# Two-layer attention kernel: two sets of accumulated sums, three buffers of low parts, and another place for the join and the first seed

## What is computed

```python
# layer 0, per image b: xf = x as [128 channels, 4096 positions]
g_x, theta_x, phi_x = g_w @ xf + g_b, theta_w @ xf + theta_b, phi_w @ xf + phi_b   # 64 channels each
y = softmax(theta_x.T @ phi_x, axis=-1) @ g_x.T
x = W_w @ y.T + W_b + xf
# layer 1, on the result
q, k, v = Wq @ xf + bq, Wk @ xf + bk, Wv @ xf + bv                                 # 128 channels
x = x + (softmax(q.T @ k / sqrt(128), axis=-1) @ v.T).T
```

## Time and profile before

| | us |
|---|---|
| median of 3 runs | 3351.05 |
| lowest and highest | 3350.34, 3352.49 |
| the profiled execution | 3353.0 |
| its span, first to last instruction | 3351.2 |
| PE busy / POOL busy in it | 3245.4 / 2854.9 |

### The profile page before, as it was taken

One profiled execution on the slowest core, in us unless ns is written; L12 is line 12 of the kernel. 1 busy time (PEld: TensorE's weight loads), 2 busy tenths in 40 slices (PEclk: granted clock), 3 DMA queues, 4 the chain that ended last, 5 costly groups with the idle time before them and its releaser, 6 DMA issues. The chain is left out here.

```text
span 3351.2 us, 38415 instructions
## 1 busy us (share of the span) xinstructions
PE 3245.4 (97%) x13636; PEld 2198.1 (66%) x13636; DVE 2094.0 (62%) x3036; ACT 1902.4 (57%) x2473; POOL 2854.9 (85%) x1419
## 2 busy tenths in 40 slices
PE   8999999999999999999999999999999999999997
PEld 5555555557777765555777776555677777677775
DVE  5555555557767665555767675555677767677773
ACT  4455455556666655555666665545565666656564
POOL 6888888888888889898888888888888888888886
PEclk9999999999999999999999999999999999999998
DMA  1000000004656640000665653000165656556565
GB/s 52 24 20 26 23 26 26 26 26 101 136 116 136 128 97 19 24 26 26 133 131 113 138 113 88 26 23 26 37 135 110 140 123 132 120 109 137 107 132 110
DMA packets 64271, 271.41 MB, mean 81 GB/s; under 512 B 7120, under 2 KB 7120, under 8 KB 39504
## 3 DMA queue, kind: packets, MB, share of 16 engines
q0 software_dynamic: 27648, 201.34, 29.7%
q1 hardware_dynamic: 36432, 67.62, 6.7%
HBM read 50.83 MB, written 16.78 MB: 20 GB/s over the span
## 5 line engine op out<-in xcount | busy, mean ns | idle before, releaser
L921 DVE TENSOR_REDUCE piece_max<-rough 128x1 f32<-128x512 f32 x2032 | 1315.7, 684 | 654.3 <-PE rough L509 648.1
L384 POOL TENSOR_TENSOR sums<-sums,probs 128x1024 f32<-128x1024 f32 x448 | 1066.3, 2380 | 139.3 <-ACT probs L838 100.9
L1040 POOL TENSOR_TENSOR p_lo<-probs,p_hi 128x1024 fp32r<-128x1024 f32 x448 | 1135.9, 2668 | 11.2 <-ACT probs L832 11.1
L938 DVE TENSOR_TENSOR probs<-scores,shift_rows 128x1024 f32<-128x1024 f32 x512 | 626.4, 1223 | 541.9 <-PE scores L542 539.6
L838 ACT ACTIVATE probs<-scores 128x1024 f32<-128x1024 f32 x512 | 520.6, 1024 | 684.2 <-PE scores L536 683.7
L831 ACT ACTIVATE p_hi<-probs 128x1024 fp32r<-128x1024 f32 x448 | 474.4, 1059 | 586.9 <-DVE probs L938 586.8
L509 PE MATMUL rough<-keys_a,qry_a 128*128 128x512 f32 x2032 | 706.6, 416 | 35.5 <-DVE piece_max L921 20.0
L509 PEld LDWEIGHTS rough<-keys_a,qry_a 128*128 128x128 f32 x2032 | 368.1, 188 | 349.8 <-DVE piece_max L921 219.3
L832 ACT ACTIVATE probs<-probs 128x1024 f32<-128x1024 f32 x512 | 535.9, 1047 | 99.1 <-DVE probs L938 99.1
L538 PE MATMUL scores<-qry_a,keys_a 128*128 128x512 f32 x1024 | 448.8, 438 | 0.0
L533 PE MATMUL scores<-qry_a,keys_a 128*128 128x512 f32 x1024 | 432.5, 422 | 0.0
(11 more groups left out here) (94 smaller groups left out, 3183.7 us busy)
## 6 DMA issues: line engine op xcount, KB each, us to landing
sent_sums<-probs POOLq DMA_DIRECT2D x192, 1024.0 KB, 6.9
x_q<-x SPq DMA_DIRECT2D x32, 256.0 KB, 2.7
x_res<-x SPq DMA_DIRECT2D x32, 256.0 KB, 3.0
mid<-mid_new SPq DMA_DIRECT2D x32, 256.0 KB, 2.3
x_kv<-mid SPq DMA_DIRECT2D x32, 256.0 KB, 2.7
x_q<-mid SPq DMA_DIRECT2D x32, 256.0 KB, 2.7
x_res<-mid SPq DMA_DIRECT2D x32, 256.0 KB, 5.4
out<-result SPq DMA_DIRECT2D x32, 256.0 KB, 5.2
```

The lines of the kernel that those rows point to most:

```text
L384: eng.tensor_tensor(sums[:], sums[:], probs[:, slot(st, s)], ALU.add).then_inc(s_plus, 1)
L921: nc.vector.reduce_max(piece_max[:, t, c:c + 1], src, AX.X).then_inc(s_reduced, 1)
L938: nc.vector.tensor_tensor(probs[:, slot(st, s)].rearrange("p (h c) -> p h c", c=QB), scores[:, s % 2].rearrange("p (h c) -> p h c", c=QB), ...
L1040: nc.gpsimd.tensor_tensor(dst, w, rd(hi), ALU.subtract).then_inc(done, 1)
```

## The change

It does four things.

- `sent_sums` exists twice, for even and for odd blocks (`st.parity`). Seeds, sends and the fold take the block's own pair. A seed waits for the fold of two blocks before in place of the one before. Layer 0's `sums` is now the first half of the even pair, and its first add waits for a fold where the block before is of layer 1.
- `p_lo` has three buffers (`LO_BUFS`), taken in the order of the split groups, and each split waits for `s_used`: PE must have used the group three splits back.
- The fold between two layer-1 blocks stands at step 3, not 2.
- The first seed stands at step 1, not 2.

```diff
@@ -22,6 +22,7 @@
 SHARED_BUFS = 2
+LO_BUFS = 3
 HI_SLOTS = (2, 3, 0, 1)
...
-FOLD_AT = {None: (None, None), 0: (1, 1), 1: (3, 2)}
+FOLD_AT = {None: (None, None), 0: (1, 1), 1: (3, 3)}
...
-SEED_AT = {2: 0, 3: 2}
+SEED_AT = {1: 0, 3: 2}
...
-        p_lo = sb("p_lo", [P, len(HI_SLOTS), GC], F32R)
+        p_lo = sb("p_lo", [P, LO_BUFS, GC], F32R)
...
-        sums = sb("sums", [P, GC])
-        sent_sums = sb("sent_sums", [P, TPG, GC])
+        sent_sums = sb("sent_sums", [P, 2, TPG, GC])
+        sums = sent_sums[:, 0, 0]
...
+        def lo_part_of(nth, s):
+
+            return p_lo[:, (halved(nth, s) - 1) % LO_BUFS]
...
-        def fold(eng, layer, g, nth):
+        def fold(eng, layer, g, nth, parity):
...
-                eng.tensor_tensor(sent_sums[:, 0], sent_sums[:, 0], sent_sums[:, 1], ALU.add).then_inc(s_join, 1)
+                both = sent_sums[:, parity]
+                eng.tensor_tensor(both[:, 0], both[:, 0], both[:, 1], ALU.add).then_inc(s_join, 1)
...
             if s == 1:
-                if st.prev == 0:
-                    eng.wait_ge(s_fold, st.g)
+                if st.prev is not None:
+                    eng.wait_ge(s_fold, st.g - (st.prev == 1))
...
-                    mm(acc_out[:, parity], hi, p_lo[:, s % len(HI_SLOTS), at], start=False, stop=False)
+                    mm(acc_out[:, parity], hi, lo_part_of(nth, s)[:, at], start=False, stop=False)
...
             def split_probs(st, s):
                 pool.wait_ge(s_whole, whole_of(st.g, s))
-                lo_part(p_lo[:, s % len(HI_SLOTS)], probs[:, slot(st, s)], hi_part(s), s_p_lo)
+                n = HALVED.index(s) - LO_BUFS
+                if n >= 0:
+                    pool.wait_ge(s_used, used(st.g, HALVED[n]))
+                elif st.prev == 1:
+                    pool.wait_ge(s_used, used(st.g - 1, HALVED[n]))
+                lo_part(lo_part_of(st.nth, s), probs[:, slot(st, s)], hi_part(s), s_p_lo)
 
             def seed(st, s):
 
                 pool.wait_ge(s_whole, whole_of(st.g, s + 1))
-                if st.prev == 1:
+                if st.prev == 0:
                     pool.wait_ge(s_fold, st.g)
-                nc.gpsimd.tensor_tensor(sent_sums[:, s // 2], probs[:, slot(st, s)], probs[:, slot(st, s + 1)],
+                else:
+                    pool.wait_ge(s_fold, st.g - 1)
+                nc.gpsimd.tensor_tensor(sent_sums[:, st.parity, s // 2], probs[:, slot(st, s)], probs[:, slot(st, s + 1)],
                                         ALU.add).then_inc(s_seed, 1)
...
-                nc.gpsimd.dma_start(sent_sums[:], probs[:, first:first + TPG], accum_op=ALU.add).then_inc(s_sent, 16)
+                nc.gpsimd.dma_start(sent_sums[:, st.parity], probs[:, first:first + TPG], accum_op=ALU.add).then_inc(s_sent, 16)
```

More of the change, by code:

```diff
@@ L365, in fold @@
                 eng.wait_ge(s_sent, sent(nth, GROUPS - 1))
-                eng.tensor_tensor(sent_sums[:, 0], sent_sums[:, 0], sent_sums[:, 1], ALU.add).then_inc(s_join, 1)
+                both = sent_sums[:, parity]
+                eng.tensor_tensor(both[:, 0], both[:, 0], both[:, 1], ALU.add).then_inc(s_join, 1)
                 eng.wait_ge(s_join, nth + 1)
-                halves = sent_sums[:, 0, 0:QB], sent_sums[:, 0, QB:GC]
+                halves = both[:, 0, 0:QB], both[:, 0, QB:GC]
             eng.wait_ge(s_den, g + 1)
@@ L378, in add @@
             if s == 1:
-                if st.prev == 0:
-                    eng.wait_ge(s_fold, st.g)
-                eng.tensor_tensor(sums[:], probs[:, slot(st, 0)], probs[:, slot(st, 1)], ALU.add).then_inc(s_plus, 1)
+                if st.prev is not None:
+                    eng.wait_ge(s_fold, st.g - (st.prev == 1))
+                eng.tensor_tensor(sums, probs[:, slot(st, 0)], probs[:, slot(st, 1)], ALU.add).then_inc(s_plus, 1)
                 return
             eng.wait_ge(s_plus, added(st.nth, s - 1))
-            eng.tensor_tensor(sums[:], sums[:], probs[:, slot(st, s)], ALU.add).then_inc(s_plus, 1)
+            eng.tensor_tensor(sums, sums, probs[:, slot(st, s)], ALU.add).then_inc(s_plus, 1)
         def halved(nth, s):
@@ L1028, in block_program @@
                 if st.ends:
-                    fold(dve, st.layer, st.g, st.nth)
+                    fold(dve, st.layer, st.g, st.nth, st.parity)
                     reciprocals(st.g, st.parity)
@@ L1098, in block_program @@
                     if s == FOLD_AT[st.prev][st.layer]:
-                        layer, g, nth, _ = before(st)
-                        fold(pool, layer, g, nth)
+                        layer, g, nth, parity = before(st)
+                        fold(pool, layer, g, nth, parity)
                     if st.layer == 0:
```

## The result

| | before | after |
|---|---|---|
| median of the runs (us) | 3350.7 (3349.26 to 3352.49) | 3386.4 (3379.53 to 3386.82) |
| ratio, with its 95% interval | | 1.0101 (1.0084 to 1.0119) |
| profiled execution (us), span | 3353.0, 3351.2 | 3379.5, 3377.7 |

The change makes the kernel 1% slower. The forecast was 3353 with a range up to 3369, so it was wrong; the time is that of its first rival (3385), which had a chance of 0.10. The profiled execution of after is the fastest of its runs, so the two spans differ by 26.5 us where the medians differ by 35.7.

What follows compares the result with a forecast made beforehand. The prediction took the loop of POOL and DMA to set the pace, with PE hanging on it. Its terms, -0.7 - 6.2 + 4.6 + 0 + 4.2 = +1.9 us, gave a median forecast of 3353, range 3334 to 3369.

Steps and rivals of the forecast that it cites:

- first rival: PE's wait at step 5 is not absorbed: each of 28 settled blocks pays 1.14 us, 32 in all, 3385; chance 0.10.
- What bounds the kernel: At layer-1 block boundaries and sends, the loop of POOL and DMA sets the pace, and PE, 97% busy, hangs on it.
- The join's wait, -0.7: On POOL, one join of 31 waits for a transfer; the second pair of sums removes that 0.7 us, once.
- The boundary, -6.2: Send 14 to send 4 on POOL: 0.22 us less than 18.85 at each of 28 boundaries, -6.2 us.
- `total` at T0 + 14.05 and PE 1.14 us late at step 5: T0 is the issue of send 14; `total` ends 14.05 after it, not 11.71, so PE waits 1.14 us longer per settled block.
- PE's wait for split 15: At step 2, PE arrives 1.1 us later and the 0.75 us wait goes; low-part waits fall from 47.7 to about 20.
- Three buffers, 0: Low-part splits on POOL also wait for PE's use three splits back: taken as 0, bounds zero to 4.2 us.
- "Is this absorbed?", +4.6: At send 8, 0.98 us of slack against 1.14 plus 0.22: 0.38 late in 12 of 28 blocks, +4.6 us.
- the two terms: The costs forecast for send 8 starting late, +4.6 us, and for transfers sharing the engines, +4.2 us.
- Transfer collisions, +4.2: Later loads and stores, such as `x_q` inside send 12, lengthen sends by 0.15 us in 28 blocks; bounds -10 and +20.
- +20: Upper bound of the transfer term and rival 2: all blocks pay 0.7 us for collisions, 3369; chance 0.15.
- deciding sign: Sign for the first rival: most sends of a block start 0.62 behind ACT instead of 0.54 behind a landing.

Runs made afterwards that it cites:

- the run with `total` behind send 4: Changed kernel with the old POOL order, but in 20 blocks `total` goes behind send 4 and PE reads it at step 7; 3336.7 us, ratio 0.9962.
- old-order run: Changed kernel with only the order tables set back (fold and first seed at step 2); doubled sums, three buffers and added waits stay; 3350.0 us, ratio 1.0004.
- run with five fillers: Changed kernel with the old POOL order, plus five extra 128x512 matmuls on PE at step 5 ahead of the products of `total`; 3371.8 us, ratio 1.0061.
- filled wait: Changed kernel, new order kept, plus five extra 128x512 matmuls on PE ahead of its wait for `total` at step 5; 3372.7 us, ratio 1.0075.
- second trace: The changed kernel itself, unaltered, measured and traced again; 3384.3 us, ratio 1.0107.
- products at the end of step 5: Changed kernel, new order kept, with PE's four products of `total` moved behind the values of group 2 and the rough pieces; 3348.6 us, ratio 0.9995.

## Why the prediction was wrong

- **What bounds the kernel** (right in part). The loop of POOL and DMA sets the pace: the run with `total` behind send 4 takes 1.75 us out of the boundary and the kernel is faster, though PE is busy 97% of it. But PE has little room either: 1.15 us more on PE alone, with POOL's list untouched, costs 21.8 us.
- **The join's wait, -0.7, and the second set as such** (right): no join waits in the changed kernel; without the new order the ratio is 1.0004.
- **The boundary, -6.2** (right): -7.0, and 18.64 in place of 18.85 in the block shown.
- **`total` at T0 + 14.05 and PE 1.14 us late at step 5** (right): 14.06, and 26 waits of 1.12 on the mean (29.1 by 26). PE's wait for split 15 shrank less than forecast: L564 fell to 40.1 us, not 20, so of the lateness PE kept most. What reaches ACT is 1.3 us.
- **Three buffers, 0** (right): no split waits for PE in the table of waits, and the old-order run, which has three buffers, is as fast as before.
- **"Is this absorbed?", +4.6** (this step failed, in two ways). Its first error is the size of the slack. The mechanism was right, send 8 starts behind ACT, but I took it in 12 of 28 blocks and with the landing of send 6 standing still. In 24 blocks send 8 starts more than 0.75 behind the landing (7 before), and the sum is 13.9, not 4.6. Part of it is the landing itself: send 6's transfers are 6.9 us shorter over all (7.08 us on the mean, 7.29 before), so the wait for ACT begins earlier. Net of that, send 8 passes on 7.0 us. I had held the loads and stores fixed against send 6 in this step, and moved them in the next. The run with five fillers prices the whole of this lateness, transfers included, at 21.8 us.
- The second error is as large again: by the runs, lateness and its transfers cost 21.8 us where the two terms had 8.8, and the clock 12 more where the prediction had nothing. No term, rival or bound of the prediction holds the clock: **idling isn't only lateness**. In 7 blocks of the one trace and 11 of the other the wait of about 1 us is followed by 3.4 us or more at half clock, and send 6, whose `probs` were done 2.3 us ahead of it in a settled block of before, now starts up to 2.5 behind the landing. This delay of send 6 is 10.2 us in the one trace and 15.2 in the other. The filled wait shows it as a cause: same lateness, no idling, 12 us less.
- **Transfer collisions, +4.2** (mechanism right, size wrong): +9.3, inside the bounds (-10 to +20). They did move from earlier sends to later ones: sends 6 and 8 are 10.5 us shorter in all, sends 10 and 12 are 18.5 us longer. Of this, 11.5 is send 12, of which the prediction said "Afterwards `x_q` will lie inside send 12". Where `x_q` is issued 1 us or more ahead of send 12, the send takes 6.89 us (the median of both traces); where it comes later, 7.67 before and 7.70 after. The late ones were 16 of 29 before and are 25 now, nine more, where I had taken a fifth of a hit in each block. The Trainium skill says that all issuing engines' transfers share the 16 engines and interleave ("DMA: Bandwidth & Descriptors", Issuing engines are not separate DMA queues). The prediction had worked out +20 from it; the traces agree that they disturb each other, and lie between. No run moves one load or store by itself, so which of them costs what is read from traces, not shown.
- **The rivals.** The first gave the time, 3385, and two thirds of the cause; that the number fits is luck. It had each of 28 blocks pay 1.14 (32 us) because PE gives nothing back. The run with five fillers shows what pure lateness costs, 21.8 us, so a third of it is absorbed, and the 12 us of the clock make up for that. Its deciding sign, that "most sends of a block start 0.62 behind ACT", isn't there: 46 of 192 sends wait for ACT. Right was that PE "has little idle to give back".

The sum with the measured terms: -7.0 - 1.1 + 7.0 (send 8 net) + 10.2 (send 6) + 16.2 (the transfers without send 6's) = +25.3, where the prediction had +1.9. What stays open: why the half clock follows in 7 of 26 waits (11 of 27 in the second trace) and not in the others, as the waits are alike (1.00 in block 52, 1.04 in block 60, which kept full clock).

## What to carry to other kernels

When an order moves a result behind one more instruction, look at who reads it: here a wait of 1 us on a busy TensorE, which looked absorbed, cost two thirds of its length in the loop, and more in clock. The cure can be on the reader's side and free: moving four small products behind 1.4 us of work that doesn't need them removed the whole loss. And the second buffer paid only once an instruction was moved past the transfer that it sets free; by itself it was worth nothing, with `total` moved behind send 4 it was worth 14 us.

## What the runs showed of the hardware

A short wait of PE can be followed by a stretch at half clock although the engine had been at full clock and busy for long. In block 20 of the changed kernel (T0 = 989.19) and in blocks 39 and 50; windows of PE with the wait in the first, and half clock in the others:

```profile
1000.30:1003.70 3.40, 2.38 (x13) 1.00 0.00 0
1004.30:1007.70 3.40, 3.40 (x6) 0.50 0.02 5
2014.80:2018.10 3.30, 3.30 (x5) 0.50 0.02 5
2547.30:2550.60 3.30, 3.30 (x8) 0.51 0.00 0
```

Such a stretch lasts 3.4 us (6.8 in block 56), and PE gets through about half as much in it. Behind the wait stand the small products of `total`, 1.02 us in all at two columns each (the trace counts eight for the program's four); they are there in every run, and all 19 of these stretches (7, 11, and 1 in the filled run) follow a wait for `total`; without the wait none came at this place. Nor does every such wait bring one: waits of 1.28 us with the products at the end of step 5, and of 2.6 us with `total` behind send 4, were not followed by one. The Trainium skill knows a clock that goes back and forth when PE idles for moments between groups of matmuls ("TensorE: Matmul & The Clock Gate", A second HAM failure mode: psum-queue depth-cycling). The traces agree, and show it here for single waits of 1.0 us, and that filling the wait with work that is thrown away is faster than idling (3372.7 against 3384.3 us, side by side on one chip).
